# A transformer block with routed experts: the token list from one-hot matmuls, the routing over all tiles at once, eight early shared chunks

## The chip, the cores and the metric

The kernel runs on one core of a Trainium2 chip. The metric is the device time of one execution in microseconds (us). The engines are TensorE (PE in the profile, PEld for its weight loads), VectorE (DVE), ScalarE (ACT), GpSimd (POOL) and SyncE (SP), which issues transfers. They run their own programs side by side and wait for one another on semaphores. DMAs are issued by SP, ACT and POOL. TensorE's clock is granted at one of two levels, 2.4 GHz (1.00 in the profile) or 1.2 GHz (0.50).

## What is computed

x is 4 x 1024 tokens of 512 channels. First an attention block with ReLU features and adaptive layernorm, then a feed-forward block with 8 experts, of which each token takes 2, and a shared expert:

```python
X = x.reshape(-1, D)                                   # T = 4096 tokens, D = 512
scores = jax.nn.sigmoid(jnp.einsum('td,ed->te', X, gate_w))
_, idx = jax.lax.top_k(scores + router_bias[None, :], 2)
w = jnp.take_along_axis(scores, idx, axis=1)
w = w / jnp.clip(jnp.sum(w, axis=-1, keepdims=True), 1e-12)
gate_full = jnp.zeros((T, E)).at[jnp.arange(T)[:, None], idx].set(w)
h1 = jnp.einsum('td,edh->eth', X, W1)                  # 8 experts, h = 352
h3 = jnp.einsum('td,edh->eth', X, W3)
y = jnp.einsum('eth,ehd->etd', jax.nn.silu(h1) * h3, W2)
out = jnp.einsum('etd,te->td', y, gate_full) + shared  # shared expert: the same form, h = 704
```

All matrix products run in split f16: each f32 operand is a high and a low f16 part, and each product is three matmuls (lines 75, 76, 77).

## The kernel before

The 4096 tokens are 32 tiles of 128. The kernel has four stages, each engine's program written out by hand in the order in which it runs.

*Attention.* One slot per tile, with LAG = 8 between the two halves. It ends with a tail of 11 slots in which shared steps already run, two per slot (steps 0 to 21).

*Shared chunks and weights.* The shared expert runs over 16 chunks of two tiles (256 tokens), in six steps each; step q is part j = q % 6 of chunk n = q // 6. `up(q)` on TensorE makes two 128x256 products (24 matmuls, 12 for j = 5) in one of three PSUM banks; `activate(q)` on ScalarE, `multiply(q)` on VectorE, `high(q)` on ScalarE and `low(q)` on VectorE turn them into split f16. `down(n)` on TensorE (34 matmuls of 512 columns) follows `up` of the third step of chunk n+1, and `add` on VectorE evacuates it. `high` of a chunk's first step waits for the down of the chunk before, whose operands it overwrites. EARLY = 10 chunks stand before the experts, 6 behind them. The weights of the 8 experts are 88 pieces (11 per expert: eight of 352 columns, three of 512): a load on ScalarE's queue in a ring of four (`w_load`), the high part on ScalarE (`w_high`, line 1013), the low part on VectorE (`w_low`, line 662). From step 22 each step does two pieces, so that they end in step 54. `w_high(p)` begins with `w_load(p + 3)`, which waits for the low part of piece p - 1.

*Routing.* In steps 22 to 27 VectorE finds the two best experts of each token (`find_top`, `find_index`, `weigh`), TensorE counts ranks with a triangular matmul and one of ones (in step 25), and VectorE works out each token's slot (`add_runs`, `place`) and each slot tile's expert (`name_tiles`). A slot list has 71 tiles of 128, each of one expert. GpSimd then scatters token number and weight of each token into a table in DRAM, 64 indirect transfers of 128 rows of 8 bytes (line 449). SP loads the table (`slot_tab`, line 305) once all have landed and its shared steps are issued.

*Experts.* For 71 slot tiles GpSimd gathers the rows (line 455), SP transposes them, TensorE runs `e_up`, `e_turn`, `e_down`, and ScalarE writes the weighted result, which SP stores. GpSimd's gathers go into the buffer of the weight stage, so they wait for all 88 pieces.

*Late stage.* The remaining chunks, with the routed sums of all 32 tiles: GpSimd gathers two rows of y per token (line 473) and adds them (line 479); tiles of late chunks take them in `add`, tiles of early chunks in `combine` on VectorE (two operations), placed in steps of the late chunks by `early_turn`.

Of the kernel before, what the change touches and what calls it, by code (L numbers as in the profile page):

```python
# [44 lines left out]
EARLY = 10  # L45
# [5 lines left out]
CONSTS = 8  # L51
GB_LOADS = 16 * (4 + B)
# [76 lines left out]
def sync_program(nc, m, sp):  # L129
# [86 lines left out]
    def shared_step(q):  # L216
# [19 lines left out]
    for s in range(-3, TILES + TAIL):  # L236
# [114 lines left out]
def gpsimd_program(nc, m, pool):  # L351
# [54 lines left out]
    for s in range(-3, TILES + TAIL):  # L406
        t = s - LAG
        if s == 0:
            step(pool.memset(m.zero[:, :], 0))
# [1226 lines left out]
```

## Time and profile before

| | |
|---|---|
| runs | 1435.37, 1439.48, 1442.59 us; median 1439.48 |
| profiled execution | 1446.23 us, span of its instructions 1444.4 us |
| TensorE | 1249.8 us busy, 87% of the span, 8990 matmuls |
| VectorE, ScalarE, GpSimd | 661.2, 415.7, 479.6 us busy |
| mean granted clock of TensorE | 0.934 |

All times in the profile count from the start of the span. A busy time is the sum of an engine's instructions. Matmuls overlap, so their single durations are longer than the distance from one to the next. "Idle before, releaser" is how long the engine had stood idle and what ended it; "issue" means that nothing which the profile shows was waited for. A line such as L75 is a line of the kernel.

### The profile page before, as it was taken

The page shows a single profiled execution, that of the slowest core. Times are in us where ns is not written, and L with a number is a line of the kernel's source. Part 1 is how long each engine was busy: PE and PEld are TensorE (multiplying, and loading weights), DVE is VectorE, ACT ScalarE, POOL GpSimd, SP SyncE. Part 2 cuts the span into 40 slices and gives each one's busy share as a digit, 9 for nine tenths or more (in the row PEclk, how much of TensorE's full clock was granted, in tenths as well). Part 3 has the DMA queues.
Part 4 walks back from the last instruction along what each step waited for, and adds up shares of the span by engine and source line. Part 5 has one row for each costly group of instructions (what it writes and reads, how often), then busy time and mean ns, then how long its engine had stood idle before and what let it go on. Part 6 is the DMA issues. An engine that isn't in the chain of part 4 may idle for free.

```text
span 1444.4 us, 25152 instructions
## 1 busy us (share of the span) xinstructions
PE 1249.8 (87%) x8990; PEld 788.6 (55%) x8990; DVE 661.2 (46%) x1376; ACT 415.7 (29%) x869; POOL 479.6 (33%) x460
## 2 busy tenths in 40 slices
PE   6997998998997989662488699999999999988896
PEld 2645665665665556440256456556565666565563
DVE  4555777777866556551145311111111111145764
ACT  2432443434433324230133212222222222211121
POOL 1213555555643322067400101111111111067661
PEclk9998999999998999885599899999999999989998
DMA  5724786987878577142135345655556555477773
GB/s 183 226 44 116 171 196 162 210 213 168 204 190 239 148 193 206 55 110 63 50 114 151 116 105 129 134 127 139 133 132 132 132 132 132 110 235 231 214 237 118
DMA packets 270067, 220.33 MB, mean 153 GB/s; under 512 B 190640, under 2 KB 203184, under 8 KB 269436
## 3 DMA queue, kind: packets, MB, share of 16 engines
q1 hardware_dynamic: 242424, 159.65, 43.8%
q0 software_dynamic: 12848, 35.47, 9.3%
q10 hardware_dynamic: 14680, 23.62, 5.7%
q8 instruction: 79, 1.29, 0.4%
q14 instruction: 36, 0.29, 0.1%
HBM read 117.29 MB, written 57.61 MB: 121 GB/s over the span
## 4 chain that ended last, share of the span: by engine, by line
PE 52%; issue 13%; DVE 10%; DMA 10%; POOL 9%; ACT 3%; SPq 3%; ACTq 1%; DVEq 0%; POOLq 0%
PE ps_o L75 6%; PE ps_vs L75 5%; PE ps_o L76 5%; PE ps_o L77 5%; PE ps_vs L76 5%; PE ps_vs L77 5%; DMA xt<-g 4%; PE ps_kh L75 2%; PE ps_kh L76 2%; PE ps_kh L77 2%; POOL ol L394 2%; DMA wp_raw<-in_wproj_t 2%; POOL h L381 1%; POOL xg L389 1%; PE ps_qh L75 1%
## 5 line engine op out<-in xcount | busy, mean ns | idle before, releaser
L455 POOL DMA_INDIRECT g<-h_d,slot_tab x71 | 67.1, 945 | 472.4 <-DMA xt<-g 352.1
L75 PE MATMUL ps_o<-w_all,xt 128*128 x568 | 179.6, 316 | 19.4 <-DMA xt<-g 19.3
L76 PE MATMUL ps_o<-w_all,xt 128*128 x568 | 179.5, 316 | 0.0
L77 PE MATMUL ps_o<-w_all,xt 128*128 x568 | 179.2, 316 | 0.0
L861 DVE SCALAR_TENSOR_TENSOR a<-ps_o,a 128x352 f32<-128x352 f32 x71 | 37.2, 524 | 183.3 <-PE ps_o L77 183.3
L866 DVE TENSOR_TENSOR at<-ps_y,at 128x384 f16<-128x384 f32 x71 | 39.6, 557 | 176.3 <-ACT at L1105 176.3
L75 PE MATMUL ps_kh<-s_ht,sh 128*128 128x256 f16 x256 | 79.5, 310 | 43.3 <-DVE s_act L620 30.4
L1110 ACT ACTIVATE y<-ps_vs,slot_tab 128x512 f32<-128x512 f32 x71 | 48.8, 687 | 230.5 <-PE ps_vs L77 230.5
L75 PE MATMUL ps_qh<-ht,wqkv 128*128 128x128 f16 x512 | 90.4, 223 | 2.5 <-DVE wqkv L613 2.5
L370 POOL TENSOR_TENSOR h<-cen,rows_f 128x512 f32<-128x512 f32 x32 | 40.6, 1268 | 154.4 <-ACT cen L904 143.0
L76 PE MATMUL ps_qh<-ht,wqkv 128*128 128x128 f16 x512 | 90.4, 223 | 0.0
L77 PE MATMUL ps_qh<-ht,wqkv 128*128 128x128 f16 x512 | 90.3, 223 | 0.0
L632 DVE TENSOR_TENSOR s_at<-s_act,s_at 128x256 f16<-128x256 f32 x80 | 40.9, 512 | 106.7 <-ACT s_at L996 106.7
L76 PE MATMUL ps_kh<-s_ht,sh 128*128 128x256 f16 x256 | 79.6, 311 | 7.9 <-issue 7.9
L473 POOL DMA_INDIRECT yb<-y_d,slot x64 | 66.0, 1031 | 60.9 <-DMA y_d<-y 25.8
L77 PE MATMUL ps_kh<-s_ht,sh 128*128 128x256 f16 x256 | 79.4, 310 | 7.6 <-issue 7.6
L449 POOL DMA_INDIRECT table<-tab_src,entry x64 | 65.6, 1026 | 60.7 <-DVE entry L832 40.7
L75 PEld LDWEIGHTS ps_o<-w_all,xt 128*128 128x128 f16 x568 | 55.9, 98 | 49.5 <-issue 22.8
L75 PE MATMUL ps_vs<-w_all,at 128*128 (+1 forms) x213 | 80.9, 380 | 0.0
L77 PE MATMUL ps_vs<-w_all,at 128*128 (+1 forms) x213 | 80.6, 379 | 0.0
L76 PE MATMUL ps_vs<-w_all,at 128*128 (+1 forms) x213 | 80.6, 378 | 0.0
L77 PE MATMUL ps_vh<-s_ht,sh 128*128 128x256 f16 x256 | 71.1, 278 | 5.0 <-issue 5.0
(225 smaller groups left out, 3267.5 us busy)
## 6 DMA issues: line engine op xcount, KB each, us to landing
y_d<-y SPq DMA_DIRECT2D x71, 256.0 KB, 3.4
w_stage<-in_w_d ACTq DMA_DIRECT2D x64, 176.0 KB
xb<-in_x SPq DMA_DIRECT2D x32, 256.0 KB, 3.3
xr<-in_x SPq DMA_DIRECT2D x32, 256.0 KB, 4.2
x_d<-x SPq DMA_DIRECT2D x32, 256.0 KB, 3.5
h_d<-hl SPq DMA_DIRECT2D x32, 256.0 KB, 2.7
h2t_d<-h2t SPq DMA_DIRECT2D x32, 256.0 KB, 3.7
s_ht<-h2t_d SPq DMA_DIRECT2D x32, 256.0 KB
```

Of the source, the lines that this page charges most:

```text
L75: nc.tensor.matmul(out, lh, rh, start=first, stop=False, skip_group_check=True)
L76: nc.tensor.matmul(out, lh, rl, start=False, stop=False, skip_group_check=True)
L77: return nc.tensor.matmul(out, ll, rh, start=False, stop=last, skip_group_check=True)
L370: pool.tensor_tensor(m.h[:, i % 2, :], m.cen[:, i % 2, :], m.rows_f[:, (i // BT) % 2, SA, :], ALU.add).then_inc(m.h_done, 1)
L394: pool.tensor_tensor(m.ol[:, t % 2, 1, :], m.o_sb[:, t % 2, :], m.ol[:, t % 2, 0, :], ALU.subtract).then_inc(m.o_lo, 1)
L449: pool.indirect_dma_start(m.table, bass.IndirectOffsetOnAxis(ap=m.entry[:, k, t:t + 1], axis=0), m.tab_src[:, k, t, :], None).then_inc(m.s ...
L455: pool.indirect_dma_start(m.g[:, t % 2, :], None, m.h2_d, bass.IndirectOffsetOnAxis(ap=m.slot_tab[:, t, 0:1], axis=0)).then_inc(m.gathered ...
L473: pool.indirect_dma_start(m.yb[:, r, k, :], None, m.y_d, bass.IndirectOffsetOnAxis(ap=m.slot[:, k, order[i]:order[i] + 1], axis=0)).then_i ...
L632: v.tensor_tensor(m.s_at[:, j, 1, :], m.s_act[:, q % 2, :], m.s_at[:, j, 0, :], ALU.subtract).then_inc(m.at_lo, 1)
L861: v.scalar_tensor_tensor(out=m.a[:, t % 2, 0:INTER], in0=m.ps_h3[:, 0:INTER], scalar=1.0 / SCALE, in1=m.a[:, t % 2, 0:INTER], op0=ALU.mult ...
L866: v.tensor_tensor(m.at[:, t % 2, 1, :, :], m.ps_a[:, :, :], m.at[:, t % 2, 0, :, :], ALU.subtract).then_inc(m.e_at_lo, 1)
L1110: act.activation(m.y[:, t % 2, :], m.ps_ey[:, 0:C], ACT.Copy, scale=m.slot_weight[:, t, 1:2]).then_inc(m.ey_ready, 1)
```

## The change

- The scattered table goes, with its zeroing at the start, its 64 scatters and its load. In its place the slot list is built in PSUM: for each tile and choice (64 pairs) VectorE makes two one-hot matrices (`pair`): token to lane, 128x128, and token to slot tile times four values (tile number, token in tile, high and low part of the weight), 128x284; TensorE multiplies them into one accumulator. Pairs are made and used in steps 26 to 36, six a step, in a ring of eight. `list_tokens` reads the list out in step 37.
- The two best experts are found with reductions over all tiles at once (`pick`), and the eight scans become one. The routing takes steps 22 to 25, the ranks are counted in step 23.
- From piece 22 on, the low part is a subtraction on GpSimd, and ScalarE scales the staged piece in place before it.
- EARLY is 8, not 10. The 66 pieces from 22 on are spread over steps 22 to 47. Piece 66 and later ones wait for the list, since the routing's buffers lie where the last two experts' weights go. The third load of the gate rows in `shared_step` goes.

```diff
-EARLY = 10
+EARLY = 8
@@ w_turn(q)
-    first = TAIL_STEPS + 2 * (q - TAIL_STEPS)
-    return range(min(first, E * WP), min(first + 2, E * WP))
+    left, steps, i = E * WP - TAIL_STEPS, EARLY_STEPS - TAIL_STEPS, q - TAIL_STEPS
+    return range(TAIL_STEPS + left * i // steps, TAIL_STEPS + left * (i + 1) // steps)
@@ gpsimd_program
-    for t in range(TILES):
-        for k in range(TOP):
-            pool.indirect_dma_start(m.table, bass.IndirectOffsetOnAxis(ap=m.entry[:, k, t:t + 1], axis=0),
-                                    m.tab_src[:, k, t, :], None).then_inc(m.scattered[k], 16)
+    def w_low(p):
+        _, dst, rows, cols = w_piece(m, p)
+        pool.wait_ge(m.w_hi, p + 1)
+        pool.wait_ge(m.w_scaled, p - TAIL_STEPS + 1)
+        pool.tensor_tensor(dst[:, 1, :], m.w_stage[0:rows, p % W_RING, 0:cols], dst[:, 0, :], ALU.subtract).then_inc(m.w_lo, 1)
@@ vector_program
+    def pick():
+        v.wait_ge(m.scores_ready, 1)
+        v.wait_ge(m.r_consts, PICKED)
+        step(v.tensor_tensor(m.sel[:, :, :], m.scores[:, :, :], m.bias[:, :].unsqueeze(1).to_broadcast([P, TILES, E]), ALU.add))
+        for k in range(TOP):
+            step(v.reduce_max(m.best[:, :], m.sel[:, :, :], AX.X))
+            step(v.tensor_tensor(m.cand[:, :, :], m.sel[:, :, :], m.best[:, :].unsqueeze(2).to_broadcast([P, TILES, E]), ALU.is_equal))
...
+        v.tensor_tensor(m.both[:, :, :], m.choice[:, 0, :, :], m.choice[:, 1, :, :], ALU.add).then_inc(m.both_ready, 1)
@@ vector_program
+    def pair(n):
+        t, k, r = n // TOP, n % TOP, n % PAIR_RING
+        at_least(v, m.pair_used, n - PAIR_RING + 1)
+        v.tensor_scalar(m.lane_is[:, r, :], m.lane_no[:, :], m.part[:, 0, k, t:t + 1], None, ALU.is_equal).then_inc(m.pair_ready, 1)
+        v.scalar_tensor_tensor(out=m.tile_is[:, r, :, :], in0=m.tile_no[:, :, :], scalar=m.part[:, 1, k, t:t + 1],
+                               in1=m.values[:, k, t, :].unsqueeze(1).to_broadcast([P, SLOT_TILES, 4]),
+                               op0=ALU.is_equal, op1=ALU.mult).then_inc(m.pair_ready, 1)
@@ vector_program, the steps from 22 on
     for q in range(TAIL_STEPS, EARLY_STEPS):
         multiply(q)
+        for n in pair_turn(q):
+            pair(n)
         low(q - 1)
         for work in beside.get(q, ()):
             work()
         if down_due(q):
             add(q // SH_TILES - 1)
-        for p in w_turn(q):
-            w_low(p)
+        if q == LIST_STEP:
+            list_tokens()
@@ scalar_program, w_high
+        staged = m.w_stage[0:rows, p % W_RING, 0:cols]
+        act.activation(dst[:, 0, :], staged, ACT.Copy, scale=SCALE).then_inc(m.w_hi, 1)
+        if p >= TAIL_STEPS:
+            act.wait_ge(m.w_hi, p + 1)
+            act.activation(staged, staged, ACT.Copy, scale=SCALE).then_inc(m.w_scaled, 1)
@@ tensor_program, the steps from 22 on
         if down_due(q):
             down(q // SH_TILES - 1)
+        for n in pair_turn(q):
+            pe.wait_ge(m.pair_ready, 2 * n + 2)
+            nc.tensor.matmul(m.ps_list.rearrange("p t n -> p (t n)"), m.lane_is[:, n % PAIR_RING, :], m.tile_is[:, n % PAIR_RING, :, :].rearrange("p t n -> p (t n)"),
+                             start=n == 0, stop=n == PAIRS - 1, skip_group_check=True).then_inc(m.pair_used, 1)
```

## Rows read from the trace of the kernel before

**Rows 1.** Busy time by stretch: us, engines busy (instructions), clock, DMA share, GB/s.
```profile
649.00:709.00 60.00, 11.86 (x35) 3.40 (x34) 7.06 (x13) 4.03 (x9) 43.31 (x44) 0.53 0.16 40
709.00:827.00 118.00, 95.44 (x655) 65.35 (x654) 53.53 (x112) 40.76 (x100) 1.94 (x2) 0.90 0.43 128
827.00:1264.00 437.00, 428.68 (x2584) 258.30 (x2585) 78.94 (x145) 107.50 (x211) 65.18 (x69) 0.99 0.57 128
1264.00:1444.00 180.00, 147.96 (x1004) 101.98 (x1002) 103.21 (x149) 28.98 (x81) 106.63 (x96) 0.91 0.66 208
```

**Rows 2.** Timeline of TensorE: start us, us, line, tile, idle before and its releaser.
```profile
596.10 0.39 PE L1297 MATMUL ps_o<-both,before 128*128 128x256 f16 x1 [12.22 <-DVE both L795]
...
685.63 0.37 PE L75 MATMUL ps_kh<-s_ht,sh 128*128 128x256 f16 x1 [2.43 <-issue]
...
688.43 0.37 PE L76 MATMUL ps_kh<-s_ht,sh 128*128 128x256 f16 x1 [2.43 <-issue]
...
827.14 0.47 PE L75 MATMUL ps_o<-w_all,xt 128*128 x1 [11.22 <-DMA xt<-g]
```

**Rows 3.** The line of the scatters: duration ns min/median/max, first and last start.
```profile
L449 POOL DMA_INDIRECT table<-tab_src,entry x64: 954/958/1497, 620.6 to 705.2; - x64
```

**Rows 4.** Busy time in stretches of 5 us, columns as in group 1.
```profile
595.00:600.00 5.00, 3.90 (x19) 2.78 (x20) 4.21 (x13) 0.00 (x0) 0.00 (x0) 0.50 0.07 23
...
600.00:605.00 5.00, 5.00 (x26) 2.50 (x24) 0.86 (x2) 0.77 (x2) 0.00 (x0) 0.92 0.18 52
...
730.00:735.00 5.00, 5.00 (x48) 4.48 (x46) 3.76 (x7) 1.84 (x4) 0.00 (x0) 1.00 0.36 104
...
735.00:740.00 5.00, 1.95 (x19) 1.52 (x18) 3.19 (x7) 1.71 (x5) 0.00 (x0) 1.00 0.68 226
...
750.00:755.00 5.00, 5.00 (x24) 2.02 (x22) 0.51 (x2) 0.00 (x0) 0.00 (x0) 1.00 0.04 15
```

**Rows 5.** Timeline of GpSimd, the first gather for the experts.
```profile
820.38 0.98 POOL L455 DMA_INDIRECT g<-h_d,slot_tab  x1 [114.22 <-DMA slot_tab<-table]
```

**Rows 6.** Timelines of ScalarE and VectorE, one piece of weights at 738.
```profile
738.40 0.50 ACT L1013 ACTIVATE w_all<-w_stage 128x352 f16<-128x352 f32 x1 [0.41 <-DVE w_all L662]
...
738.93 0.52 DVE L662 SCALAR_TENSOR_TENSOR w_all<-w_stage,w_all 128x352 f16<-128x352 f32 x1 [0.29 <-ACT w_all L1013]
...
739.48 0.33 ACTq L1002 DMA_DIRECT2D w_stage<-in_w_d  x1
...
739.86 0.50 ACT L1013 ACTIVATE w_all<-w_stage 128x352 f16<-128x352 f32 x1 [0.97 <-DVE w_all L662]
```

**Rows 7.** Instructions by line and shape: count, busy us, mean ns, idle before.
```profile
L1013 ACT ACTIVATE w_all<-w_stage 128x352 f16<-128x352 f32 x64 | 31.6, 494 | 58.6 <-DVE w_all L662 52.1 <-DMA w_stage<-in_w_d 3.8 <-issue 2.7
...
L1013 ACT ACTIVATE w_all<-w_stage 128x512 f16<-128x512 f32 x16 | 10.1, 628 | 17.2 <-DVE w_all L662 16.4 <-issue 0.6 <-DMA w_stage<-in_w_d 0.2
...
L1100 ACT ACTIVATE a<-ps_o 128x352 f32<-128x352 f32 x71 | 32.9, 464 | 98.6 <-PE ps_o L77 98.6
...
L394 POOL TENSOR_TENSOR ol<-o_sb,ol 128x512 f16<-128x512 f32 x32 | 38.4, 1201 | 18.4 <-ACT ol L941 18.4
...
L880 DVE TENSOR_TENSOR yb<-yb,gb 128x512 f32<-128x512 f32 x20 | 13.7, 685 | 9.1 <-POOL yb L479 9.1
...
L883 DVE TENSOR_TENSOR xc<-yb,xc 128x512 f32<-128x512 f32 x20 | 19.3, 963 | 0.7
```

**Rows 8.** Timeline of VectorE, products and low parts of a shared step.
```profile
737.89 0.42 DVE L620 SCALAR_TENSOR_TENSOR s_act<-ps_kh,s_act 128x256 f32<-128x256 f32 x1
...
738.23 0.41 DVE L632 TENSOR_TENSOR s_at<-s_act,s_at 128x256 f16<-128x256 f32 x1
...
1286.83 2.15 DVE L632 TENSOR_TENSOR s_at<-s_act,s_at 128x256 f16<-128x256 f32 x1
```

**Rows 9.** Timeline of ScalarE, first high part after a down.
```profile
782.69 0.42 ACT L996 ACTIVATE s_at<-s_act 128x256 f16<-128x256 f32 x1 [5.68 <-PE ps_vs L1250]
...
1363.02 0.42 ACT L996 ACTIVATE s_at<-s_act 128x256 f16<-128x256 f32 x1 [7.50 <-PE ps_vs L1250]
...
1389.71 0.42 ACT L996 ACTIVATE s_at<-s_act 128x256 f16<-128x256 f32 x1 [8.61 <-PE ps_vs L1250]
```

More of the change, by code:

```diff
@@ L50 @@
 W_COLS = W13_COLS + IT * 2 * C
-CONSTS = 8
-GB_LOADS = 16 * (4 + B)
+CONSTS = 5
+PAIRS = TOP * TILES
+PAIR_RING = 8
+PAIRS_PER_STEP = 6
+PAIRS_FROM = TAIL_STEPS + 4
+PICKED = 4
+BIG = 1e30
+LIST_STEP = PAIRS_FROM + (PAIRS + PAIRS_PER_STEP - 1) // PAIRS_PER_STEP
+GB_LOADS = 16 * (3 + B)
 MODS = 6
@@ L639, in add @@
             v.wait_ge(m.sy_done, i + 1)
-            if n < EARLY and n in (0, 8):
-                v.wait_ge(m.s_gb_loaded, 48 if n == 0 else 64)
+            if n == 0:
+                v.wait_ge(m.s_gb_loaded, 48)
             v.wait_ge(m.act_done, SH_TILES * (n + 1))
@@ L802, in weigh @@
         for k in range(TOP):
-            step(v.scalar_tensor_tensor(out=m.tab_weight[:, k, :, 1], in0=m.weight[:, k, :], scalar=1.0 / SCALE, in1=m.wsum[:, :],
+            step(v.scalar_tensor_tensor(out=m.weight[:, k, :], in0=m.weight[:, k, :], scalar=SCALE, in1=m.wsum[:, :],
                                         op0=ALU.mult, op1=ALU.mult))
+        step(v.tensor_copy(m.values[:, :, :, 2], m.weight[:, :, :]))
+        step(v.tensor_tensor(m.values[:, :, :, 3], m.weight[:, :, :], m.values[:, :, :, 2], ALU.subtract))
     rank = m.ps_r[:, 0, :].rearrange("p (t e) -> p t e", e=E)
     total = m.ps_r[:, 1, :].rearrange("p (t e) -> p e t", e=E)
-    run = m.top[:, :, :].rearrange("p t e -> p (t e)").rearrange("p (e t) -> p e t", e=E)
+    run = m.run
     def add_runs():
         v.wait_ge(m.ranks_done, 2)
-        for e in range(E):
-            step(v.tensor_tensor_scan(run[:, e, :], m.onesf[:, :], total[:, e, :], 0.0, ALU.mult, ALU.add))
+        v.wait_ge(m.r_consts, 6)
+        step(v.tensor_copy(m.totals[:, :, :], total))
+        step(v.tensor_tensor_scan(run[:, :, :].rearrange("p e t -> p (e t)"), m.carry[:, :, :].rearrange("p e t -> p (e t)"),
+                                  m.totals[:, :, :].rearrange("p e t -> p (e t)"), 0.0, ALU.mult, ALU.add))
         step(v.tensor_scalar(m.padded[:, :], run[:, :, TILES - 1], float(P - 1), None, ALU.add))
@@ L817, in add_runs @@
         step(v.tensor_copy(m.padded[:, :], m.count_i[:, :]))
[L818 removed]
+        step(v.tensor_tensor_scan(m.ends[:, :], m.carry[:, 0, 1:1 + E], m.padded[:, :], 0.0, ALU.mult, ALU.add))
         step(v.tensor_tensor(m.starts[:, :], m.ends[:, :], m.padded[:, :], ALU.subtract))
     def place():
[L822 to L824 removed]
+        step(v.tensor_tensor(run[:, :, :], run[:, :, :], m.totals[:, :, :], ALU.subtract))
+        step(v.tensor_tensor(run[:, :, :], run[:, :, :], m.starts[:, :].unsqueeze(2).to_broadcast([P, E, TILES]), ALU.add))
+        step(v.tensor_tensor(m.sel[:, :, :], rank, run[:, :, :].rearrange("p e t -> p t e"), ALU.add))
         for k in range(TOP):
@@ L1451, in place_buffers @@
     m.sct_rep = region(BACK_AT + (QT_RING - 1) * 2 * GRP * P * 2, END)("sct_rep", [P, KC, P], F32)
-    m.zero = sb("zero", [P, 2 * SLOT_TILES], I32)
     sb = region(SHARED_AT, W_STAGE_AT)
```

145 lines of the change are left out of this document (72 added, 73 removed).

## Prediction

> **What bounds the kernel now.** I read the busy time by stretch first. It splits the profiled execution (span 1444.4 us, time 1446.23) into attention (to 577), shared chunks 3 to 9 with the routing and the weight conversion (577 to 827), the experts (827 to 1264) and six late shared chunks with the combining (1264 to 1444). TensorE is 98% busy among the experts, but has 11.9 us of work in the 60 us from 649 to 709, at a granted clock of 0.53 [rows 1]. The timeline of TensorE says what stops it there: nothing that the profile can name ("issue"), one 256-column matmul every 2.8 us [rows 2]. The 64 scatters of the old table run from 620.6 to 705.2 [rows 3], and the pace returns 3 us after the last. So a stall of some 57 us goes with them: the 35 matmuls of the stretch would take 3.7 us at the pace of 48 in 5 us [rows 4].
>
> The question is what is late next. The gather for the experts starts at 820.38 [rows 5], and TensorE's first expert matmul comes at 827.14, after 11.22 us of waiting [rows 2]. The change must be judged by when that matmul comes, and by what two more late chunks cost.
>
> **Removed.** 64 scatters, the table's store and load, the 32 MAX8 and 32 FIND_INDEX8 and eight scans. Without the scatters nothing else in the rows would hold the old order: -57 us, if nothing else took their place. The zero table and the constants at the kernel's start lie beside the weight splits of the first tiles: 0, a gain of 1 us at the most, their issue.
>
> **The pieces of weights.** 66 of 88 pieces fall into the steps that change. Each piece is a serial round, because the load of piece p+3 stands ahead of the conversion of piece p in ScalarE's program and waits for piece p-1's low part. Before, the round is ScalarE 0.50 (738.40), VectorE 0.52 (738.93), issue of the load 0.38 (739.48), and the next piece at 739.86: 1.46 us [rows 6]. After it is: load issue 0.38, high part 0.49, the new scaling pass on ScalarE, the subtraction on GpSimd, and four hand-overs of 0.03 (738.90 to 738.93). The scaling pass is nearest to the 128x352 f32 activation, 0.46; scaled by columns to 512, 0.67. The subtraction on GpSimd is nearest to ol, 128x512 f16 out of f32 and f16, 1.20; by columns 0.83 for 352 (bounds 0.7 and 1.2) [rows 7]. A narrow piece then takes 0.38+0.49+0.46+0.83+0.12 = 2.28, a wide one 0.38+0.63+0.67+1.20+0.12 = 3.00; of eleven pieces three are wide, so 27.2 us for an expert, 2.48 a piece, and 66 pieces take 164 us at least (150 to 190 by the bounds). ScalarE's activation and high part of each step fit beside GpSimd's subtraction. They are also packed into 26 steps, 2.54 a step: 6.3 us a step against 2.6 of TensorE's (24 matmuls at 48 in 5 us [rows 4]).
>
> **The pairs.** In steps 26 to 36 VectorE makes six pairs a step (four in the last) after `multiply(q)`, and TensorE takes them after `up(q)`, before `up(q+1)`. Before, TensorE ran ahead of the other engines, as far as three PSUM banks let it; now it can't, as pairs of step q wait for `multiply(q)`, and this for `activate(q)`, and this for `up(q)`. Queued behind the waiting pair matmuls are `up(q+1)`, every `down`, and through them ScalarE. A pair is an operation of 128 and one of 284 columns. Two 256-column operations follow one another at 0.34 (737.89, 738.23) and last 0.42 and 0.41 [rows 8], so 0.5 to 0.8 a pair; I take 0.65, or 3.9 a step. A step is then the round activate 0.4, multiply 0.4, pairs 3.9, the last matmul 0.2, `up(q+1)`. For `up` the clock counts: after a wait of 12.22 us [rows 2] TensorE's next stretch had a granted clock of 0.50 (the level of 1.2 GHz), and the one after 0.92, nearly all of it at 2.4 GHz [rows 4]. In the pair steps it idles 4.9 us but for six small matmuls, then works. I take `up` at the lower clock for 4.3 us (20 matmuls) and the rest at the higher: 4.75, a round of 9.65 (7.6 at the higher clock all along). The half-width `up` of a chunk's last step makes its round 7.4.
>
> **The downs.** `high(6n)` waits for `down(n-1)`, which stands behind `up(6n+2)`: 34 matmuls at 24 in 5 us [rows 4] with their gaps, 7.6 us. ScalarE waited 5.68 us for one of them before [rows 9]. With TensorE a step behind instead of ahead, ScalarE now waits through multiply, pairs, a whole `up` and the down in step 31, and no piece is converted.
>
> **The sum of the stretch**, on the clock of the profile:
> - GpSimd and ScalarE start pieces at 582. Ten pieces, 25 us, and a wait for `down(3)`, 6 us (the routing's 13 operations before the ranks take 0.45 each, 0.41 [rows 8] and a wait, so the ranks come at 588; then three `up`, the first at the lower clock, 10, and the down, 7.6): step 26 at 613.
> - Steps 26 to 30: 4 x 9.65 + 7.4 = 46, to 659.
> - Step 31: 4.9 for multiply and pairs, 4.75 `up(32)`, 7.6 down, then three pieces 7.4: 24.6, to 683.5.
> - Steps 32 to 35: 3 x 9.65 + 7.4 = 36.4, to 720; step 36 with four pairs 8.4, to 728.
> - Step 37: `up(38)` and down 10.2, two pieces 5, to 743.5. The list is made under it; the wait of piece 66 for it (step 39) costs nothing.
> - Steps 38 to 47: 26 pieces 64.5, one down 7, less 3 as the last pieces wait for no load: to 812.
> - Gather and transpose as before, 820.38 to 827.14, 6.8 [rows 2, 5]: first expert matmul at 819, 8 us earlier than 827.14.
>
> So of the 57 us little is left: two fewer chunks and no scatters are paid for by slower pieces and by coupled steps. The ranks, list and names on VectorE (13, 10, 9 and 13 small operations) lie beside ScalarE's pieces, which are later. The 64 pair matmuls cost TensorE 0.12 to 0.24 each, within the round.
>
> **The late stage.** The experts are untouched, 437 us [rows 1]. A late chunk takes 26.7 us (the high part after a down at 1363.02 and at 1389.71 [rows 9]), with VectorE's `add`, then multiplies and combines, on the path. Two more: +53. The six old late chunks hold 3, 3, 4, 3, 3, 4 combines, the eight new ones two each: 8 fewer where time is counted, each 0.69 and 0.96 us of VectorE [rows 7], a third to all of it on the path: -5 to -13, I take -9. So +44 (38 to 50). GpSimd's fetching, 107 us of 180 [rows 1], stays in all.
>
> Span: 1444.4 - 8 + 44 = 1480.4, time 1482; the median run stands 6.75 us under the profiled one (1439.48 against 1446.23): **1475 us**.
>
> **A rule of the skill.** VectorE's second operand from SBUF meets GpSimd's reads: the same 128x256 subtraction took 0.41 us with GpSimd idle and 2.15 beside its sums [rows 8]. The Trainium skill says the same and goes further ("SBUF — State Buffer", section "Who interferes with whom"): the pair of ports is a lock for the whole instruction, and the second to come blocks in full. By it every second operation of a pair and every `low` may wait for a GpSimd subtraction, and the other way round; that is the fourth rival. In the sum I have only 0.1 a pair for it, as GpSimd works 28 x 0.93 = 26 us of the 115 of the pair steps.
>
> **Rivals.**
> - *TensorE keeps its higher clock in the pair steps*: each `up` 2.6 and not 4.75, some ten of them: 20 us less, 1455. For it: from 735 to 740 TensorE worked 1.95 of 5 us and kept a clock of 1.00 [rows 4]. Against it: these gaps are longer than that one and come in every step, and from 649 to 709, with sparse matmuls only, the clock was 0.53 [rows 1].
> - *The pieces alone set the stretch* (TensorE does not fall behind; this ends on the other side): 582 + 164 + 7 for the last gather + 12 for four downs = 765, so -62 + 44 = -18: 1421. It decides if a pair costs under 0.3 us, as the round then falls below the pieces' 6.3. Against it: the program order, and 0.33 at least from one operation to the next.
> - *The late stage gives more back*: less fetching per chunk, 24 us a chunk, with the higher clock above: 1441, no change.
> - *The lock*: in 11 steps up to three subtractions of 0.83 hold up pairs: +27, 1502.
> - *The change does not remove the stall*, if it was TensorE's instruction stream and not the scatters: about 1530. Against it: its end with the last scatter [rows 2, 3].
>
> **How the numbers follow.** Forecast 1475, chance 0.42; higher clock 1455, 0.22; lock 1502, 0.15; pieces alone 1421, 0.10; late stage 1441, 0.08; stall stays 1530, 0.03. A measurement of this kernel tells about 0.5%, 7 us, from no change: below 1432 is faster, 0.10; to 1447 the same, 0.08; above, slower, 0.82. The range leaves out the fastest case and the last and takes in the others with the bounds of the pieces and of the late stage: 1440 to 1508.
>
> **What would show it.** In the profile after: no "issue" gaps near 650; GpSimd's low parts at 0.83 and 1.2 us, 2.3 to 3.0 from one to the next; TensorE waiting for the pairs of each step from 613 to 728 and its clock near 0.5 to 0.7 there; first expert matmul near 819; 26 us a late chunk. I am wrong if pairs cost 0.3, if the clock holds, or if late chunks take 23.

## The result, and the profile after

| | before | after |
|---|---|---|
| median of the runs | 1438.87 us (4 runs) | 1493.92 us (4 runs, 1487.99 to 1498.21) |
| profiled execution, span | 1446.23, 1444.4 us | 1498.21, 1496.4 us |
| mean granted clock of TensorE | 0.934 | 0.928 |

The ratio is 1.038, 95% interval 1.0335 to 1.0424: slower, as forecast, by more than forecast (1475). Three marks cut each trace into stages: the first activation of step 22 (start of the stretch that changes), the first expert matmul, and the last slot tile's output on ScalarE (end of the experts).

| us | step 22 starts | shared chunks, routing, weights | experts | late stage | span |
|---|---|---|---|---|---|
| before | 580.2 | 246.9 | 441.3 | 176.0 | 1444.4 |
| after | 582.0 | 247.2 | 442.9 | 224.3 | 1496.4 |
| forecast of after | 580.2 | 238.8 | 441.3 | 220.0 | 1480.4 |

So the middle stretch, which has twelve steps and 64 scatters less, takes as long as before, and the late stage has grown by 48. The busy time of the new kernel by stretch, to be held against [rows 1]. Columns: us, busy us of PE, PEld, DVE, ACT and POOL (instructions), granted clock, DMA share, GB/s.

```profile
582.00:613.00 31.00, 18.41 (x108) 11.68 (x108) 20.29 (x48) 12.08 (x27) 8.40 (x13) 0.83 0.24 71
613.00:740.00 127.00, 75.67 (x336) 42.05 (x337) 67.10 (x166) 38.44 (x82) 34.44 (x30) 0.69 0.24 69
740.00:829.00 89.00, 45.70 (x289) 29.86 (x286) 19.59 (x37) 37.78 (x81) 28.69 (x31) 0.76 0.34 97
829.00:1272.00 443.00, 432.70 (x2615) 261.36 (x2616) 79.97 (x147) 108.47 (x213) 65.20 (x69) 0.99 0.56 127
1272.00:1496.00 224.00, 188.04 (x1305) 129.95 (x1302) 122.74 (x175) 37.19 (x104) 108.46 (x96) 0.93 0.55 171
```

From 613 to 740, the pair steps, TensorE is 60% busy at a clock of 0.69 and no other engine is over 53%: none is the bound, they wait for one another in turn. The groups of instructions by line, from 582 to 829, say for what. TensorE's matmuls of the pairs have the largest idle time of the stretch in front of them, and GpSimd's low parts (narrow and wide) wait for ScalarE's scaling pass. No group of TensorE in this stretch has "issue" among its releasers any more.

```profile
L1335 PE MATMUL ps_o<-tile_is,lane_is 128*128 128x284 f16 x64 | 23.6, 368 | 55.6 <-DVE tile_is L848 55.6
...
L457 POOL TENSOR_TENSOR w_all<-w_stage,w_all 128x352 f16<-128x352 f32 x48 | 45.9, 957 | 136.6 <-ACT w_stage L1045 136.4
L457 POOL TENSOR_TENSOR w_all<-w_stage,w_all 128x512 f16<-128x512 f32 x12 | 15.0, 1248 | 24.0 <-ACT w_stage L1045 24.0
```

ScalarE's timeline gives the pace: the activations of steps 26, 27 and 28, and the high part that stands behind the down in step 31.

```profile
615.80 0.36 ACT L1010 ACTIVATE s_act<-ps_qh 128x256 f32<-128x256 f32 x1
...
627.59 0.38 ACT L1010 ACTIVATE s_act<-ps_kh 128x256 f32<-128x256 f32 x1 [5.96 <-PE ps_kh L84]
...
637.80 0.38 ACT L1010 ACTIVATE s_act<-ps_vh 128x256 f32<-128x256 f32 x1 [3.53 <-PE ps_vh L84]
...
685.48 0.42 ACT L1024 ACTIVATE s_at<-s_act 128x256 f16<-128x256 f32 x1 [17.29 <-PE ps_vs L1282]
```

VectorE and GpSimd in the same steps: the two operations of an undisturbed pair take 0.28 and 0.51, and the next pair begins 0.61 after it. The first operation of the third pair, beside a GpSimd subtraction that began just before it (619.04), takes 1.20. A low part that takes 0.85 alone takes 3.86 where it begins inside a run of six pairs (647.78 to 651.5). That is the extreme: the other 20 narrow ones between steps 26 and 37 take 0.85 to 1.64.

```profile
617.84 0.28 DVE L847 TENSOR_SCALAR lane_is<-lane_no,part 128x128 f16<-128x128 f32 x1
618.03 0.51 DVE L848 SCALAR_TENSOR_TENSOR tile_is<-tile_no,part,values 128x284 f16<-128x284 f32 x1
618.45 0.28 DVE L847 TENSOR_SCALAR lane_is<-lane_no,part 128x128 f16<-128x128 f32 x1
...
619.04 1.15 POOL L457 TENSOR_TENSOR w_all<-w_stage,w_all 96x512 f16<-96x512 f32 x1 [1.85 <-ACT w_stage L1045]
619.08 1.20 DVE L847 TENSOR_SCALAR lane_is<-lane_no,part 128x128 f16<-128x128 f32 x1
...
648.77 3.86 POOL L457 TENSOR_TENSOR w_all<-w_stage,w_all 128x352 f16<-128x352 f32 x1 [5.72 <-ACT w_stage L1045]
...
654.21 0.85 POOL L457 TENSOR_TENSOR w_all<-w_stage,w_all 128x352 f16<-128x352 f32 x1 [1.58 <-ACT w_stage L1045]
```

The first expert matmul compares with the last row of [rows 2], the two high parts of the late stage with [rows 9]: a late chunk takes 26.6 us here, 26.7 there.

```profile
829.23 0.47 PE L82 MATMUL ps_o<-w_all,xt 128*128 x1 [31.63 <-DMA xt<-g]
...
1415.88 0.42 ACT L1024 ACTIVATE s_at<-s_act 128x256 f16<-128x256 f32 x1 [8.40 <-PE ps_vs L1282]
1442.47 0.42 ACT L1024 ACTIVATE s_at<-s_act 128x256 f16<-128x256 f32 x1 [8.53 <-PE ps_vs L1282]
```

The questions for the experiments: did the stall really go with the scatters; what took its place, the pairs or the pieces; and what do two chunks cost on either side of the experts. In all of them the step-22 mark lies between 574 and 582 us, a spread that also two runs of one kernel show (580.2 and 575.5), so stages are compared from mark to mark.

### The profile page after: what moved, and what is told of

The parts are those of the page before. It is cut to its first block, busy times and chain, and to the rows that moved or that the text cites. A ratio compares the mean times of both kernels' runs of the same rounds, so it can differ in the third digit from the quotient of the medians.

```text
span 1496.4 us, 25373 instructions
## 1 busy us (share of the span) xinstructions
PE 1277.0 (85%) x9054; PEld 801.1 (54%) x9054; DVE 687.0 (46%) x1345; ACT 451.5 (30%) x935; POOL 485.4 (32%) x466
## 4 chain that ended last, share of the span: by engine, by line
PE 51%; DVE 12%; DMA 11%; POOL 10%; issue 9%; ACT 5%; SPq 2%; ACTq 1%; DVEq 0%; POOLq 0%
PE ps_o L82 5%; PE ps_vs L82 5%; PE ps_o L83 5%; PE ps_o L84 5%; PE ps_vs L83 5%; PE ps_vs L84 5%; DMA xt<-g 5%; PE ps_kh L82 2%; DVE tile_is L848 2%; PE ps_kh L83 2%; PE ps_kh L84 2%; DMA wp_raw<-in_wproj_t 2%; POOL ol L396 2%; PE ps_qh L82 2%; DMA h2t<-hl 2%
## 5 line engine op out<-in xcount | busy, mean ns | idle before, releaser
L466 POOL DMA_INDIRECT g<-h_d,slot_token x71 | 67.3, 949 | 359.1 <-DMA xt<-g 351.7
L457 POOL TENSOR_TENSOR w_all<-w_stage,w_all 128x352 f16<-128x352 f32 (+2 forms) x66 | 67.8, 1027 | 169.8 <-ACT w_stage L1045 169.7
L1142 ACT ACTIVATE y<-ps_vs,slot_weight 128x512 f32<-128x512 f32 x71 | 48.8, 687 | 230.6 <-PE ps_vs L84 230.6
L82 PE MATMUL ps_kh<-s_ht,sh 128*128 128x256 f16 x256 | 81.7, 319 | 28.3 <-DVE s_act L631 25.3
L82 PE MATMUL ps_qh<-ht,wqkv 128*128 128x128 f16 x512 | 88.6, 221 | 2.2 <-DVE wqkv L624 2.2
L83 PE MATMUL ps_qh<-ht,wqkv 128*128 128x128 f16 x512 | 88.4, 220 | 0.0
L84 PE MATMUL ps_qh<-ht,wqkv 128*128 128x128 f16 x512 | 88.4, 220 | 0.0
L83 PE MATMUL ps_kh<-s_ht,sh 128*128 128x256 f16 x256 | 81.0, 316 | 0.0
L84 PE MATMUL ps_kh<-s_ht,sh 128*128 128x256 f16 x256 | 80.7, 315 | 0.0
L1024 ACT ACTIVATE s_at<-s_act 128x256 f16<-128x256 f32 x96 | 39.1, 407 | 120.2 <-PE ps_vs L1282 120.0
## 6 DMA issues: line engine op xcount, KB each, us to landing
w_stage<-in_w_d ACTq DMA_DIRECT2D x64, 176.0 KB, 2.3
```

The costliest lines, as they stand in the source:

```text
L82: nc.tensor.matmul(out, lh, rh, start=first, stop=False, skip_group_check=True)
L83: nc.tensor.matmul(out, lh, rl, start=False, stop=False, skip_group_check=True)
L84: return nc.tensor.matmul(out, ll, rh, start=False, stop=last, skip_group_check=True)
L457: pool.tensor_tensor(dst[:, 1, :], m.w_stage[0:rows, p % W_RING, 0:cols], dst[:, 0, :], ALU.subtract).then_inc(m.w_lo, 1)
L466: pool.indirect_dma_start(m.g[:, t % 2, :], None, m.h2_d, bass.IndirectOffsetOnAxis(ap=m.slot_token[:, t:t + 1], axis=0)).then_inc(m.gathe ...
L1024: act.activation(m.s_at[0:w, j, 0, :], m.s_act[0:w, q % 2, :], ACT.Copy).then_inc(m.at_hi, 1)
```

## The scatters, and a chip without the stall

**The kernel before without its scatters.** The 64 scatters are left out, so the table stays zero and every slot gathers token 0.

```diff
-    for t in range(TILES):
-        for k in range(TOP):
-            pool.indirect_dma_start(m.table, ...).then_inc(m.scattered[k], 16)
...
-    for j in range(2):
-        sp.wait_ge(m.scattered[j], 16 * TILES)
+    sp.wait_ge(m.slots_ready, 1)
```

> The kernel before, with the 64 scatters left out (the table stays zero, so every slot gathers token 0 with weight 0; all else runs the same instructions). Theory, the stall is the scatters' own: with them gone the steps of the second stage keep the pace of their surroundings, first expert matmul at 827 - 57 = 770 us, time 1382 (ratio 0.960; 1375 to 1395). Rival, the stall belongs to TensorE's instruction stream at that place: still gaps of 2.8 us from one matmul to the next near 650, time 1439.

Measured: 1388.75 us against 1437.99, ratio 0.965 (0.9612 to 0.9684). The middle stretch takes 193.4 us in place of 246.9: the stall is worth 53.5 us there. That is the first theory, with 57 a little too high. The first expert matmul of this kernel:

```profile
767.55 0.47 PE L75 MATMUL ps_o<-w_all,xt 128*128 x1 [12.77 <-DMA xt<-g]
```

**The kernel before, again.** The experiments ran in four sets, each on a chip of its own. On the first the unchanged kernel took 1438 us, as in the profile before; on the second it took 1386. A third chip was like the second, a fourth like the first. On the third it was profiled once more, as it is.

> The kernel before, unchanged, once more with a profile: its time was 1438 in the first comparison and 1386 in the second, on another chip. Theory, the stall beside the scatters belongs to the chip: where the time is near 1386 the scatters of the old table are issued as before, but TensorE shows no gaps of 2.8 us between matmuls near 650 and its first expert matmul comes near 770; where it is near 1438 the stall stands as in the first profile. Rival, the scatters themselves are faster there, with the stall per scatter unchanged. Rival, the 51 us lie in another stage.

Measured: 1382.61 us, beside 1385.42 in 13 runs on that chip. The scatters are there as in [rows 3], as many, the first to the last start over 89 us (85 in the first profile). TensorE beside them is 81% busy (in the first profile from 620 to 709: 34.37 of 89 us, 39%), and its first expert matmul comes at 767.14.

```profile
L449 POOL DMA_INDIRECT table<-tab_src,entry x64: 954/1098/1501, 615.7 to 704.8; - x64
...
616.00:706.00 90.00, 72.61 (x500) 49.88 (x501) 46.79 (x96) 32.78 (x79) 70.08 (x64) 0.92 0.49 144
...
767.14 0.47 PE L75 MATMUL ps_o<-w_all,xt 128*128 x1 [10.91 <-DMA xt<-g]
```

Its middle stretch is 191.6 us, that of the kernel without scatters on the first chip 193.4. So the stall needs the scatters and a chip (or a state of one) that is open to it; on the third chip the scatters cost nothing. In this run no group of TensorE carries "issue" from 577 to 770. In the first profile nine do from 577 to 830, together 50.0 us of idle time (8.6, 7.9, 7.6, 4.3, 5.0, 2.5, 3.8, 3.8 and 6.5), near the difference between the two kinds of chip (1438 - 1386 = 52). Three of the nine:

```profile
L76 PE MATMUL ps_kh<-s_ht,sh 128*128 128x256 f16 x96 | 29.8, 310 | 7.9 <-issue 7.9
...
L77 PE MATMUL ps_vh<-s_ht,sh 128*128 128x256 f16 x97 | 27.3, 281 | 5.0 <-issue 5.0
...
L77 PE MATMUL ps_qh<-s_ht,sh 128*128 128x256 f16 x76 | 22.1, 290 | 6.5 <-issue 6.5
```

The stall doesn't begin with the scatters. In the first profile they start at 620.6, and from 640 to 645 TensorE is still busy all the time, at a clock of 1.00; its first gap with "issue" ends at 648.84, 28 us after the first scatter. On the fourth chip (first scatter at 616.6) the gaps begin at 637, 20 us after it.

```profile
640.00:645.00 5.00, 5.00 (x25) 2.05 (x23) 0.00 (x0) 0.00 (x0) 3.83 (x4) 1.00 0.02 1
...
648.84 0.27 PE L76 MATMUL ps_vh<-s_ht,sh 128*128 128x256 f16 x1 [0.36 <-issue]
```

**The changed kernel, again**, on the same third chip.

> The changed kernel, unchanged, once more. It has no scatters, so its time should not depend on the chip: 1494 wherever it runs; the ratio to the kernel before is 1.038 on a chip with the stall and 1494 / 1386 = 1.078 on one without. Rival, what makes the chip faster is general: 1494 - 51 = 1443 where the kernel before takes 1386.

Measured: 1492.43 us, ratio 1.0788 (1.0714 to 1.0863). It takes the same time on both kinds of chip (1493.92 in the result, where the kernel before took 1438.87), its middle stretch 246.6 and 247.2 us. The change is 3.8% slower where the old kernel stalls and 7.9% slower where it doesn't. In return its time no longer depends on the chip.

## What took the stall's place

**One pair in place of 64.** All else as in the changed kernel; 63 pairs are left out, so most slots gather token 0.

```diff
-PAIRS = TOP * TILES
+PAIRS = 1
...
-LIST_STEP = PAIRS_FROM + (PAIRS + PAIRS_PER_STEP - 1) // PAIRS_PER_STEP
+LIST_STEP = PAIRS_FROM + 11
```

> The changed kernel with 63 of the 64 pairs left out (one pair is built and multiplied; the other slots gather token 0 with weight 0). Theory, the coupled round of the pairs costs 10.4 us a step in steps 26 to 36: without it these steps are piece-bound, 28 pieces of 2.57 us and two downs, 82 us in place of 125: 1494 - 42 = 1452 (ratio 1.009). Rival, pieces alone set the stretch and pairs are hidden: 1494 (1.038). Rival, the pairs cost only their VectorE and port time, 64 x 0.65 less what is hidden, about 20 us: 1474 (1.024).

Measured: 1442.07 us (10 runs), ratio 1.0006 (0.9981 to 1.0031); the middle stretch 193.4 us, first expert matmul at 770.70. The pairs cost 247.2 - 193.4 = 53.8 us, more than the 42 of the theory, and by chance just what the scatters' stall costs (53.5). The change swaps one for the other. That both kernels stand at 193.4 without their burden is a coincidence too: one does 38 steps there and the other 26, so the slower pieces (26 us, by a run below) eat up what the twelve steps would have given.

```profile
611.00:690.00 79.00, 55.79 (x326) 36.20 (x327) 18.55 (x35) 37.42 (x82) 26.64 (x28) 0.80 0.35 109
...
770.70 0.47 PE L82 MATMUL ps_o<-w_all,xt 128*128 x1 [32.09 <-DMA xt<-g]
```

**All 64 pairs, taken two steps later.** VectorE does the same pairs in the same steps; TensorE multiplies them behind `up(q+2)` (first part of the diff), and VectorE's `low(q-1)` goes ahead of them (second part). The list is made two steps later.

```diff
-PAIR_RING = 8
+PAIR_RING = 14
+PAIR_DELAY = 2
...
-LIST_STEP = PAIRS_FROM + (PAIRS + PAIRS_PER_STEP - 1) // PAIRS_PER_STEP
+LIST_STEP = PAIRS_FROM + (PAIRS + PAIRS_PER_STEP - 1) // PAIRS_PER_STEP + PAIR_DELAY
...
-        for n in pair_turn(q):
+        for n in pair_turn(q - PAIR_DELAY):
...
+        low(q - 1)
         for n in pair_turn(q):
             pair(n)
-        low(q - 1)
```

> The changed kernel, with TensorE taking the pairs of step q two steps later (behind up(q+2)), 14 pair buffers in place of 8, and VectorE doing low(q-1) ahead of the step's pairs, so that neither up nor the next activation stands behind the pairs; the list is made two steps later. Theory, the 54 us of the pairs are the coupling (TensorE stopped a step behind): most of it goes, the steps become piece-bound at 6.5 us with 2.5 pieces, VectorE's 4.6 to 5.2 us a step under it: 1494 - 40 = 1454 (ratio 1.011). Rival, the time is the pairs' own VectorE and port time: 20 us gone at most, 1474 (1.025). Rival, the order does not matter: 1494 (1.039).

Measured on the second chip: 1441.26 us. The ratio to the kernel before there is 1.0409 (1.0362 to 1.0457), to the changed kernel 1441.26 / 1493.92 = 0.965. The middle stretch takes 196.8 us: 50.4 of the 53.8 us are gone with an edit of the order alone (and of the buffers that it needs), 3.4 are left for 64 pairs (the middle stretches of the changed kernel's two profiles differ by 0.6). Which of the two moves brings how much wasn't tried. VectorE's work is not less (67.56 us in 82, against 67.10 in 127), and the wait ahead of the pair matmuls falls from 55.6 us to 21.8. So the price was the coupling: `up(q+1)` behind matmuls that wait for VectorE's pairs, which wait for `up(q)`.

```profile
612.00:694.00 82.00, 60.54 (x334) 36.16 (x335) 67.56 (x162) 37.67 (x82) 33.34 (x28) 0.79 0.36 106
...
L1336 PE MATMUL ps_o<-tile_is,lane_is 128*128 128x284 f16 x60 | 16.5, 326 | 21.8 <-DVE tile_is L849 21.8
...
775.07 0.47 PE L83 MATMUL ps_o<-w_all,xt 128*128 x1 [31.68 <-DMA xt<-g]
```

**The clock.** TensorE gets 36 matmuls of 256 columns into an unused accumulator before it waits for the pairs of a step.

```diff
+FILL = 36
...
         for n in pair_turn(q):
+            if n % PAIRS_PER_STEP == 0:
+                for _ in range(FILL):
+                    nc.tensor.matmul(m.ps_y[:, 0:2 * P], m.sh[:, 0, 0:P], m.sh[:, 0, 0:2 * P], start=True, stop=True, skip_group_check=True)
             pe.wait_ge(m.pair_ready, 2 * n + 2)
```

> The changed kernel, with 36 matmuls of 256 columns into an unused accumulator on TensorE ahead of each step's wait for its pairs (3.9 us at the higher clock). Theory, the clock: TensorE's waits let it fall to 1.2 GHz, so that up takes 3.9 to 4.3 us and a down 5 or more; kept busy it holds 2.4 GHz, up 2.6: 1.5 us a step less in 11 steps and 4 at each of two downs, 1494 - 24 = 1470 (ratio 1.022), granted clock above 0.9 from 620 to 740. Rival, fillers begun at the lower clock take 7.7 us, delay the pairs and the step: 1494 + 20 = 1514 (1.053). Rival, TensorE's clock is not what the round waits for: 1494.

Measured: 1477.55 us, 16.4 less than the changed kernel; the middle stretch 237.4 in place of 247.2, at a granted clock of 0.90 from 610 to 730 (after: 0.69 from 613 to 740). The direction is the theory's, the size 10 us of 24: useless work at the higher clock buys a fifth of what the order buys. Between the two profiled spans lie 19.4 us; 6.2 of them lie ahead of step 22 and 3.8 among the experts, where the kernels don't differ and two profiles of one kernel lie nearly as far apart (4.9 and 5.2).

```profile
610.00:730.00 120.00, 99.99 (x737) 74.20 (x738) 65.21 (x162) 37.42 (x81) 33.31 (x29) 0.90 0.25 73
```

## The pieces of weights

**Low parts on VectorE**, in one operation as before, without the scaling pass.

```diff
-        if p >= TAIL_STEPS:
-            act.wait_ge(m.w_hi, p + 1)
-            act.activation(staged, staged, ACT.Copy, scale=SCALE).then_inc(m.w_scaled, 1)
...
-        pool.tensor_tensor(dst[:, 1, :], m.w_stage[0:rows, p % W_RING, 0:cols], dst[:, 0, :], ALU.subtract).then_inc(m.w_lo, 1)
...
+        for p in w_turn(q):
+            w_low(p)
```

> The changed kernel, with the low parts of the 66 late pieces back on VectorE in one operation, as before, and no scaling pass. Theory, the piece's round of 2.43 to 3.0 us sets the steps outside the pair steps: the round falls to 1.5, steps 38 to 47 shorten by 25 us, the three blocks of pieces ahead of step 26 and behind the downs of steps 31 and 37 by 10, and the pair steps by 8 as no pair meets GpSimd: 1494 - 43 = 1451 (ratio 1.008 to the kernel before). Rival, the pair steps and the downs set everything: 10 us, 1484 (1.031). Rival, the two shared-port engines only change places (VectorE's added 0.52 us a piece lands on the path of the pairs): no gain, 1494 or above.

Measured: 1464.39 us, ratio 1.0163 (1.0123 to 1.0202), 29.5 less than the changed kernel against 43 expected; the middle stretch 221.4 in place of 247.2 (-25.8). From step 26 to step 37 it takes 114.4 us (616.25 to 730.69) in place of 124.7 (615.80 to 740.48), so 10 less there; behind step 37 it takes 18 less, ahead of step 26 2 more. GpSimd's pieces are thus worth 26 us in the changed kernel.

With no GpSimd subtraction beside them, the 128 operations of the pairs take 50.2 us in all, and each run of six pairs 3.73. In the changed kernel they take 58.8 us, and a run of six 3.73 to 5.24. So the meeting of the two engines costs VectorE 8.6 us there, 7.3 of it in the first operation of a pair. By line and shape, from 613 to 740, first the changed kernel, then this run:

```profile
L848 DVE SCALAR_TENSOR_TENSOR tile_is<-tile_no,part,values 128x284 f16<-128x284 f32 x64 | 33.7, 527 | 0.0
L847 DVE TENSOR_SCALAR lane_is<-lane_no,part 128x128 f16<-128x128 f32 x64 | 25.1, 391 | 0.0
...
L838 DVE SCALAR_TENSOR_TENSOR tile_is<-tile_no,part,values 128x284 f16<-128x284 f32 x64 | 32.4, 506 | 0.0
L837 DVE TENSOR_SCALAR lane_is<-lane_no,part 128x128 f16<-128x128 f32 x64 | 17.8, 279 | 0.0
```

**The load behind the conversion**, with GpSimd's low parts kept.

```diff
     def w_high(p):
-        w_load(p + W_RING - 1)
+        if p < TAIL_STEPS:
+            w_load(p + W_RING - 1)
...
             act.activation(staged, staged, ACT.Copy, scale=SCALE).then_inc(m.w_scaled, 1)
+            w_load(p + W_RING - 1)
```

> The changed kernel, with the load of piece p+3 issued behind the conversion of piece p (in place of ahead of it), for the 66 late pieces: ScalarE no longer waits for GpSimd's low part of piece p-1 before it converts piece p. Theory, the round is then ScalarE's 0.50 + 0.50 + 0.38 = 1.4 us (narrow) in place of 2.43: 25 us less in steps 38 to 47, nothing in the pair steps: 1494 - 25 = 1469 (ratio 1.021). Rival, the loads then arrive late and ScalarE waits for them: 1494 or above. Rival, GpSimd's own 0.85 to 1.2 with blocked reads sets the pace: 1480 (1.029).

Measured: 1473.38 us, 20.5 less than the changed kernel; the middle stretch 232.0 (-15.2). Behind step 37 it takes 71.2 us in place of 88.7, but from step 26 to step 37 129.0 in place of 124.7, where the theory had no change: GpSimd's subtractions take longer among the pairs, the longest 3.88, 4.67 and 4.69 us. In the changed kernel two narrow pieces follow one another at 2.42 us (772.41, 774.83), ScalarE idle for 1.40 before each; here two take 3.05 us (786.24, 787.16, the next at 789.29), with a step's activation among them.

```profile
772.41 0.50 ACT L1042 ACTIVATE w_all<-w_stage 128x352 f16<-128x352 f32 x1 [1.40 <-POOL w_all L457]
...
774.83 0.50 ACT L1042 ACTIVATE w_all<-w_stage 128x352 f16<-128x352 f32 x1 [1.40 <-POOL w_all L457]
```

```profile
786.24 0.49 ACT L1043 ACTIVATE w_all<-w_stage 128x352 f16<-128x352 f32 x1
...
787.16 0.49 ACT L1043 ACTIVATE w_all<-w_stage 128x352 f16<-128x352 f32 x1
...
789.29 0.49 ACT L1043 ACTIVATE w_all<-w_stage 128x352 f16<-128x352 f32 x1
```

**The same edit in the kernel before.**

> The kernel before, with the load of piece p+3 issued behind the conversion of piece p (for the 66 pieces behind the attention), the one edit of the changed kernel's experiments that costs nothing else. Theory, ScalarE's wait for the low part of the piece before is on the path of the old kernel's chunks too (1.46 us a piece, 12 pieces a chunk of 26.8 us), but TensorE is busy 23 to 24 of these 27 us, so at most 3 us a chunk come back: 10 us over five chunks, ratio 0.993, on either kind of chip. Rival, the round is hidden behind TensorE: 1.000. Rival, the piece sets the chunk in full, 12 x 0.5 = 6 us a chunk: 30 us, 0.978.

Measured (fourth chip, with the stall): 1441.04 us against 1436.12, ratio 1.0023 (0.9999 to 1.0047): no difference. The theory of 10 us fell, the rival (hidden behind TensorE) stands. Two rounds of 1.46 us a step are covered there; 2.5 rounds of 2.43 a step, as in the changed kernel, are not. It was run only on a chip with the stall.

## Two chunks, on either side of the experts

The changed kernel with ten early chunks; the third load of the gate rows comes back with them.

```diff
-EARLY = 8
+EARLY = 10
...
-GB_LOADS = 16 * (3 + B)
+GB_LOADS = 16 * (4 + B)
...
+        if j == 0 and n % 4 == 2 and n > 4:
+            sp.wait_ge(m.s_xs_done, 2 * (n - 2))
+            sp.dma_start(m.s_gb[:, (n // 4 + 1) % 2, :], ...).then_inc(m.s_gb_loaded, 16)
```

> The changed kernel with ten shared chunks ahead of the experts again, one-hot list and GpSimd's low parts kept; the 66 pieces are spread over 38 steps. Theory, a late chunk costs 26.5 and an early one less: the late stage gives back 48 us, the twelve added steps cost about 30 (38 pieces of 2.57 us and two downs behind step 37 in place of 26 pieces): 1476 (ratio 1.026). Rival, an early chunk costs as much as a late one: 1494 (1.038). Rival, the added steps are nearly free since pieces bound the stretch: 1449 (1.007).

Measured: 1472.55 us, ratio 1.023 (1.0194 to 1.0267). The late stage takes 172.1 us in place of 224.3 (-52.2), the middle one 283.0 in place of 247.2 (+35.8): two chunks cost 16 us more behind the experts than ahead of them, in this kernel with its slow pieces. The first expert matmul and the last output of the experts:

```profile
861.99 0.47 PE L82 MATMUL ps_o<-w_all,xt 128*128 x1 [21.06 <-DMA xt<-g]
...
1298.07 0.69 ACT L1145 ACTIVATE y<-ps_vs,slot_weight 128x512 f32<-128x512 f32 x1 [1.56 <-PE ps_vs L84]
```

## Three edits together

**Ten early chunks, low parts on VectorE, pairs two steps later.** The diffs are those above.

> The changed kernel with three edits at once: ten chunks ahead of the experts, low parts of the weights on VectorE, pairs taken two steps later. Theory, the scatters' stall (50 us in the run without them) goes and nothing of its size comes in its place: near the kernel before without scatters (1389) plus 64 pairs of 0.65 us on VectorE, of which half is hidden: 1410 (ratio 0.980). Rival, VectorE with pieces, pairs and steps is the bound (11 steps of 6.5 us in place of 4.5): 1420 (0.987). Rival, the pairs stay as dear as now: 1440 (1.00).

Measured on the second chip: 1405.02 us, ratio 1.0152 (1.0103 to 1.0201), 88.9 less than the changed kernel. The middle stretch is 216.5 us. The edits don't simply add: alone they gave 21.4, 29.5 and 52.7, together 103.6. The pieces' low parts now stand behind six pairs in VectorE's program, and ScalarE waits for them.

```profile
619.91 0.50 ACT L1038 ACTIVATE w_all<-w_stage 128x352 f16<-128x352 f32 x1 [7.25 <-DVE w_all L667]
...
626.37 0.63 ACT L1038 ACTIVATE w_all<-w_stage 128x512 f16<-128x512 f32 x1 [4.37 <-DVE w_all L667]
```

**Four pairs a step, two pieces a step, the load behind the conversion**, on top of the three.

```diff
-PAIRS_PER_STEP = 6
+PAIRS_PER_STEP = 4
...
-    return range(TAIL_STEPS + left * i // steps, TAIL_STEPS + left * (i + 1) // steps)
+    first = TAIL_STEPS + 2 * (q - TAIL_STEPS)
+    return range(min(first, E * WP), min(first + 2, E * WP))
...
+        if p < TAIL_STEPS:
+            w_load(p + W_RING - 1)
...
+            w_load(p + W_RING - 1)
```

> The three edits of the run before it (ten early chunks, low parts on VectorE, pairs taken two steps later) with four pairs a step over 16 steps, two pieces a step as in the kernel before, and the load of piece p+3 behind the conversion of piece p. Theory, the pieces then wait for 2.6 us of pairs and not 3.9, and end four steps ahead of the experts: 1405 - 12 = 1393, against the kernel before 0.969 on a chip with the stall, 1.005 on one without. Rival, the pairs' VectorE time is conserved (40 us in any spread): 1405.

Measured on the third chip: 1388.63 us (10 runs) against 1385.42, ratio 1.003 (1.0004 to 1.0056); 105.3 less than the changed kernel. The middle stretch is 199.4 us, and behind the last pair TensorE is 85% busy at a clock of 0.96:

```profile
711.00:774.00 63.00, 53.33 (x393) 38.54 (x392) 35.30 (x76) 24.41 (x61) 2.15 (x2) 0.96 0.48 148
```

This kernel has no scatters. On a chip with the stall the kernel before takes 1436 to 1438, so this one should be some 48 us faster there, if it takes the same time on both kinds, as the changed kernel does; that is an estimate, and it wasn't run on such a chip. Where there is no stall, none of the kernels here beats the kernel before: the one-hot list's best is level with the scatters.

## Why the prediction was right, and where it was off

The verdict, the sign and the order of size held. The span came out 16.0 us above the forecast's 1480.4, the median 18.9 above 1475: the forecast took the profiled execution to lie 6.75 us above the median, as before, and it lay 4.3 above.

| part | forecast | measured | difference |
|---|---|---|---|
| step 22 starts later | 0 | +1.8 | 1.8 |
| middle stretch | -8.1 | +0.3 | 8.4 |
| experts | 0 | +1.6 | 1.6 |
| late stage | +44 | +48.3 | 4.3 |

- **The stall goes.** Right: no "issue" is left, 53.5 us by the run without scatters, forecast 57. What the forecast couldn't see is that the 53.5 belong to some chips only.
- **The coupled round.** Right in its mechanism, shown by the two-steps-later run (50 of 54 us come back from order and buffers). The mis-sized term is the six pairs of a step: 3.9 us were taken, 0.65 a pair with 0.1 of it for GpSimd. Measured are 3.73 undisturbed and up to 5.24 (617.84 to 623.08), on average of the ten runs of six 4.6. `up` was taken too high: 4.1 (623.42 to 627.55) and not 4.75, which cancels part of it. From step 26 (615.80) to step 27 it is 11.8 us, with a `multiply` that waited until VectorE had made the tiles' names; then 10.2, where 9.65 was taken. The short round of a half-width `up` takes 8.8 and not 7.4. Steps 26 to 30 take 52.0 us (forecast 46), steps 32 to 35 take 40.7 (36.4), step 31 with the down 23.9 (24.6). Step 37 starts at 740.5, forecast 728: without the later start of 1.8, 10.7 us are lost up to here. What lies behind gives 2.3 back (740.5 to 829.2 = 88.7, forecast 728 to 819 = 91).
- **The pieces.** Right: 0.85 and 1.15 us on GpSimd undisturbed (0.83 and 1.20 taken), 2.43 and 3.00 from one to the next (2.28 and 3.00 taken). The narrow scaling pass takes 0.50, not 0.46.
- **The downs.** Right: 17.29 us of waiting in step 31, with no piece converted.
- **The late stage.** The chunk was right (26.6). The mis-sized term is the combines given back: 53 - 9 was forecast, 2 x 26.6 - 48.3 = 4.9 measured, and only half of that is the combines' doing. In the kernel before a late chunk with three combines takes 26.7 us and the one with four 27.9 (the high parts at 1335.08, 1363.02 and 1389.71), in the middle of the changed kernel's late stage a chunk with two 26.5 to 26.8. So only a fourth combine is on the path, 1.2 us for each of two such chunks. The rest came by luck: with ten early chunks, and so as many combines as before, the one-hot kernels have late stages of 171.0 to 172.1 us, the kernel before and its two variants 176.0 to 177.6. Where these 4 to 7 us come from stays open.
- **The experts** were taken as unchanged; in all runs they lie between 436 and 445, which is more than the 1.6.

**The rivals.** The higher clock (1455) did not come: 0.69, forecast 0.5 to 0.7; forced up to 0.90 it gives 10 us in the middle stretch. "Pieces alone" (1421) needed pairs at 0.3 us, and they take 0.62. Its price was too low as well: with one pair left the middle stretch takes 193.4 us, where it had 185 (580 to 765). The late stage gave back less, not more. The lock (1502) is real and small: 27 us were forecast for this rival, and the pairs' operations take 8.6 us more than in the run with VectorE's low parts, where steps 26 to 37 are 10.3 shorter. The trace shows both directions, a pair's first half at 1.20 instead of 0.28, and a GpSimd subtraction of 3.86 that ends 1.1 us after the six pairs do. The rule of the Trainium skill ("SBUF — State Buffer", section "Who interferes with whom"), that the second to come is blocked in full, fits the 1.20: the subtraction beside it began 0.04 us earlier and lasted 1.15. By itself it does not give the 3.86, as each of VectorE's operations lasts 0.51 at most; this subtraction waited through eight of them. The 1.20 is a `tensor_scalar` with one full operand in SBUF, which the forecast had not counted among the operations that meet GpSimd; the same section lists `tensor_scalar` among those that can take both ports.

**Left open.** What makes a chip stall beside 64 small scatters isn't settled. The scatters take 954 to 1500 ns on both kinds (median 958 in the first profile, 1098 on the third chip), and the profile names nothing that TensorE waits for. In the first 20 to 28 us of the scatters it shows no such gap. From 645 to 705 the two instruction queues move one packet each in the first profile and two each on the third chip; whether that is the cause or follows from the fewer instructions isn't shown. Whether fewer scatters, or scatters further apart, would avoid the stall wasn't tried.

## What to carry to other kernels

When work is inserted into a hand-ordered pipeline, price the order before the work: the same 64 pairs cost 54 us where TensorE takes them in the step in which they are made, and 3.4 us two steps later. A stall that the profile ascribes to nothing ("issue") may be a property of the chip that was measured, so profile the kernel on a second chip before the removal of such a stall is booked as a gain. A part that lies beside other work is free only up to a bound: two pieces a step at 1.46 us each were hidden here, 2.5 a step at 2.43 were not.

## What the runs showed of the hardware

- On some chips TensorE stalls beside GpSimd's 64 scatters. Two profiles of a stalled run, the first one and that of the fourth chip (the kernel before with later loads), show it slow down 28 and 20 us after the first scatter, in the end to one 256-column matmul every 2.80 us. On the third chip the same program had no such gap. By the times of the kernel before, two of the four sets of runs had the stall and two didn't: a difference of 52 us (3.7%) in the medians. From the fourth chip:

```profile
661.52 0.37 PE L75 MATMUL ps_kh<-s_ht,sh 128*128 128x256 f16 x1 [2.42 <-issue]
664.32 0.37 PE L76 MATMUL ps_kh<-s_ht,sh 128*128 128x256 f16 x1 [2.43 <-issue]
```

- The changed kernel, without scatters, took the same on two chips (1493.92 and 1492.43).
- A `tensor_scalar` of 0.28 us on VectorE (128x128, f32 in, f16 out) took up to 1.26 where a GpSimd subtraction ran beside it (12 of the 64 in the changed kernel took over 0.3); in the run without such subtractions all 64 took 0.27 or 0.28.
- The other way round, one GpSimd subtraction of 0.85 us took 3.86: it began inside a run of twelve VectorE operations and ended only after it. With the loads moved, three took 3.88 to 4.69. It isn't the rule: another, which also began inside such a run (629.33), took 1.04, and the other 20 narrow ones in the changed kernel's pair steps took 0.85 to 1.64.
